# Expert trips of a two-layer feed-forward kernel: taken one batch at a time, spread over twelve steps, with a gelu built from tanh and GpSimd products

## The reference

```python
x = x + 0.5 * ffn(layernorm(x))      # stage 0
x = x + attention(layernorm(x))      # stage 1: relative position bias, 1024 x 1024 per head
x = x + 0.5 * ffn(layernorm(x))      # stage 2, same weights as stage 0

def ffn(x):
    x = x + attention_without_bias(layernorm(x) * ln1_w + ln1_b)
    y = layernorm(x) * ln2_w + ln2_b
    expert = argmax(y @ gate_w + gate_b)             # one of 8 experts per token
    return x + gelu_tanh(y @ w1[expert]) @ w2[expert]   # 128 -> 512 -> 128
```

## Time and profile before

| what | value |
|---|---|
| median of 3 runs | 2478.51 us (2477.31 to 2483.67) |
| the profiled execution, its time | 2486.23 us |
| its span | 2484.4 us |
| granted TensorE clock, mean | 0.924 of full speed |
| first to last exponential | 73.3 to 2368.4 us of the span |
| PE, DVE, ACT, POOL busy | 2179.9, 1935.1, 1910.1, 786.5 us (88%, 78%, 77%, 32%) |

### The profile page before, as it was taken

The page is one execution under the profiler, slowest core; times in us unless marked ns, Lnnn a source line. Parts: engine busy times, 40 slices in busy tenths (PEclk is TensorE's granted clock), DMA queues, the critical chain, the costliest instruction groups (busy, mean ns, idle before and its releaser), DMA issues. The chain is left out here.

```text
span 2484.4 us, 62352 instructions
## 1 busy us (share of the span) xinstructions
PE 2179.9 (88%) x24162; PEld 797.6 (32%) x24162; DVE 1935.1 (78%) x3222; ACT 1910.1 (77%) x3561; POOL 786.5 (32%) x1167
## 2 busy tenths in 40 slices
PE   5899988889997999999999899999889889988945
PEld 1222221225421334543233233222222223532435
DVE  7989898985788886578888888899989998569210
ACT  1788787889877777887777777788979988878822
POOL 1344634330634521042442023022061232062153
PEclk7899898899988999999999899899999999999967
DMA  4335433235304434743443333111101103622525
GB/s 112 98 104 151 127 82 90 54 91 160 83 23 110 124 99 143 214 117 93 113 115 99 101 98 102 48 36 28 39 23 42 36 15 102 173 65 60 139 78 145
DMA packets 269674, 231.91 MB, mean 93 GB/s; under 512 B 64241, under 2 KB 223857, under 8 KB 269346
## 3 DMA queue, kind: packets, MB, share of 16 engines
q1 hardware_dynamic: 258114, 219.54, 31.7%
q0 software_dynamic: 11264, 8.40, 1.9%
HBM read 175.35 MB, written 65.04 MB: 97 GB/s over the span
## 5 line engine op out<-in xcount | busy, mean ns | idle before, releaser
L1299 ACT ACTIVATE probs<-psum 128x512 f32<-128x512 f32 x3072 | 1619.1, 601 | 333.0 <-PE psum L1066 193.4
L1412 DVE TENSOR_REDUCE maxes<-psum 128x2 f32<-128x1024 f32 x1216 | 1422.5, 1215 | 267.8 <-PE psum L1034 257.2
L1103 PE MATMUL psum<-probs,v_ones 128*9 128x256 f32 (+1 forms) x11520 | 994.5, 419 | 0.0
L1066 PE MATMUL psum<-q_staged,k_staged 27*128 27x512 f16 x3072 | 809.4, 406 | 47.5 <-DMA q_staged<-neg_max 17.2
L1034 PE MATMUL psum<-k_staged,q_staged 24*128 24x512 f16 x3072 | 631.1, 409 | 160.0 <-DVE maxes L1412 124.1
L1417 DVE CUSTOM_DVE_ANT_0 biased<-psum,strips 128x512 bf16<-128x512 f32 x640 | 409.4, 686 | 103.3 <-PE psum L1034 86.4
L1034 PEld LDWEIGHTS psum<-k_staged,q_staged 24*128 24x128 f16 x3072 | 145.6, 92 | 901.5 <-DVE maxes L1412 510.4
L1103 PEld LDWEIGHTS psum<-probs,v_ones 128*9 128x9 f32 x11520 | 172.2, 89 | 332.4 <-issue 261.8
L1066 PEld LDWEIGHTS psum<-q_staged,k_staged 27*128 27x128 f16 x3072 | 222.2, 91 | 174.9 <-ACT probs L1299 84.7
L815 POOL TENSOR_SCALAR max_rest<-max_turned 128x32 f32<-128x32 f32 x96 | 28.3, 295 | 649.6 <-DVE max_turned L1455 647.4
L1086 PE MATMUL psum<-near,ident_b 64*64 64x256 bf16 (+4 forms) x3840 | 149.3, 251 | 0.0
(11 more groups left out here) (166 smaller groups left out, 1292.7 us busy)
## 6 DMA issues: line engine op xcount, KB each, us to landing
m_w<-in_w SPq DMA_DIRECT2D x204, 256.0 KB
near<-bias_near SPq DMA_DIRECT2D x128, 240.0 KB
strips<-bias_strips SPq DMA_DIRECT2D x64, 288.0 KB
k_staged<-k_parts SPq DMA_DIRECT2D x192, 48.0 KB
bias_cuts<-bias_window SPq DMA_DIRECT2D x32, 240.0 KB, 3.1
near<-bias_cuts SPq DMA_DIRECT2D x32, 240.0 KB, 3.7
bias_near<-near SPq DMA_DIRECT2D x32, 240.0 KB, 4.0
heads<-heads_t SPq DMA_DIRECT2D x384, 18.0 KB
```

The costliest lines, as they stand in the source:

```text
L1066: mm_ = pe.matmul(bank[:, :], k.kst[p][rows_, kt * P:(kt + 1) * P], queries, start=True, stop=not biased_)
L1103: last = pe.matmul(heads_bank[32 * j:32 * j + VC, columns], k.v[:, batch_of(u) * KT + kt, u % QUADS * 4 + j, :], probs[:, step % 3 * 4 + j ...
L1299: act.activation(probs[:, step % 3 * 4 + e % 4, :], bank[:, :], ACT.Exp, scale=unscale[is_mid(u)]).then_inc(taken, 1)
L1412: dve.reduce_max(maxes[u % 2][:, half, 2 * i:2 * i + 2, t, chunk], slot, AX.X).then_inc(drained, 1)
```

## The change

- Every batch of stages 0 and 2 is its own set: 8 sets of 5 trips, 40 trips in place of 34. The scatter target shrinks to 15 tiles, the normalised tokens to one batch.
- In the six sets other than the last two batches of stage 2, a trip takes 12 steps (`PITCH`). Its first-layer products come at steps 1, 3 and 5 of the trip, its second-layer products and their evictions one slot each at steps 7, 9 and 11, its weight loads at steps 6 to 8 and 12 to 14. First trips: step 117 for the first set, then 175, 239, 303, 623 and 687.
- In these trips gelu is no table function. ScalarE copies the hidden layer with a factor sqrt(0.044715); GpSimd forms x^3 + x in three instructions (`pool_cube`, one step later); ScalarE takes the tanh (`act_bend`, three steps after the copy); GpSimd multiplies and adds in two instructions (`pool_gelu`, four steps after the copy); the eviction scales by 0.25/sqrt(0.044715).
- The last two batches keep gelu and one-burst trips (`DIRECT`). The trips of batch 2 lie behind the last unit, at steps 768, 771, 776, 788 and 791; those of batch 3 stay at 810 and on.
- The gathers of stage 0 come at steps 179, 237, 301 and 365 (before: 203, 235, 331, 363); with them the projections of stage 1.
- The parts of a projection half (turn, q, k, v) come at 0, 2, 4, 6 in place of 0, 2, 3, 4. `pool_near` runs at 61, 77, 93 and 109. Two units of stage 1 lose their late loading (`LATE_UNITS`).

On ScalarE, in the second unit with trips of stage 0. The first rows are of before: a trip (m_yt, gelu m_hidden, m_out) with its two table loads.

The diff, cut to its core (the waits of the SyncE loads follow the new step tables and are left out):

```diff
-MT = 2 * KT + E
+MT = KT + E - 1
...
-BATCHES = {(0, 0): (0, 1), (0, 2): (2, 3), (2, 0): (0, 1), (2, 2): (2,), (2, 3): (3,)}
+BATCHES = {(n, b): (b,) for n in (0, 2) for b in range(B)}
...
+DIRECT = [(STAGES - 1, b) for b in (B - 2, B - 1)]
+PITCH = 12
+CUBE = 0.044715 ** 0.5
+BEND = (2 / math.pi) ** 0.5 / CUBE
...
-    return route_step(n, b) + FIRST_TRIP[len(BATCHES[n, b])] + (3 if len(BATCHES[n, b]) == 2 else 4) * trip
+    if (n, b) == DIRECT[0]:
+        return TRIPS_BEHIND[trip]
+    if (n, b) == DIRECT[1]:
+        return route_step(n, b) + FIRST_TRIP + 4 * trip
+    return route_step(n, b) + (FIRST_TRIP if (n, b) != SETS[0] else FIRST_SET_TRIP) + PITCH * trip
+
+def hidden_at(n, b, r):
+    return 1 if (n, b) in DIRECT else 1 + 2 * r
+
+def down_at(n, b):
+    return ((2, tuple(range(SLOTS))),) if (n, b) in DIRECT else tuple((7 + 2 * r, (r,)) for r in range(SLOTS))
...
-PROJECT_SINCE = {0: "p_turn", 2: "p_q", 3: "p_k", 4: "p_v"}
+PROJECT_SINCE = {0: "p_turn", 2: "p_q", 4: "p_k", 6: "p_v"}
...
-NEAR_STEPS = [8 * w + 5 for w in (WINDOWS - 1, WINDOWS + 2, WINDOWS + 5, WINDOWS + 7)]
+NEAR_STEPS = [8 * w + 5 for w in (WINDOWS - 1, WINDOWS + 1, WINDOWS + 3, WINDOWS + 5)]
...
+    def pool_cube(pool, n, b, trip, r):
+        x, power = hidden[r][:, :], bent[bend_index(n, b, trip, r) % 2][:, :]
+        pool.wait_ge(taken, seat["m_hidden", n, b, trip, r] + 1)
+        if bend_index(n, b, trip, r) >= 2:
+            pool.wait_ge(m_ready, bend_index(n, b, trip, r) - 1)
+        link(pool, pool.tensor_tensor(power, x, x, op=ALU.mult))
+        link(pool, pool.tensor_tensor(power, power, x, op=ALU.mult))
+        pool.tensor_tensor(power, power, x, op=ALU.add).then_inc(m_cubed, 1)
+
+    def pool_gelu(pool, n, b, trip, r):
+        x, curve = hidden[r][:, :], bent[bend_index(n, b, trip, r) % 2][:, :]
+        pool.wait_ge(m_bent, bend_index(n, b, trip, r) + 1)
+        link(pool, pool.tensor_tensor(curve, curve, x, op=ALU.mult))
+        pool.tensor_tensor(x, x, curve, op=ALU.add).then_inc(m_ready, 1)
...
+                if (n, b) not in DIRECT and since == 1:
+                    pool_cube(pool, n, b, trip, r)
+                if (n, b) not in DIRECT and since == 4:
+                    pool_gelu(pool, n, b, trip, r)
...
+    def act_hidden(act, n, b, trip, r):
+        bank = take(act, "m_hidden", n, b, trip, r)
+        if (n, b) in DIRECT:
+            act.activation(hidden[r][:, :], bank[:, :], ACT.Gelu_apprx_tanh).then_inc(taken, 1)
+        else:
+            act.activation(hidden[r][:, :], bank[:, :], ACT.Copy, scale=CUBE).then_inc(taken, 1)
+
+    def act_bend(act, n, b, trip, r):
+        act.wait_ge(m_cubed, bend_index(n, b, trip, r) + 1)
+        curve = bent[bend_index(n, b, trip, r) % 2][:, :]
+        act.activation(curve, curve, ACT.Tanh, scale=BEND).then_inc(m_bent, 1)
```

More of the change, by code:

```diff
@@ L172 @@
 LAST_STEP = gather_step(2, B - 1) + 8
-DOWN_STEPS = {trip_step(*key) + 2: [key] for key in TRIP_KEYS}
-LATE_UNITS = [(B + b) * QUADS for n, b in SETS if n == 0]
+DOWN_STEPS = {}
+for key in TRIP_KEYS:
+    for since, slots in down_at(*key[:2]):
+        DOWN_STEPS.setdefault(trip_step(*key) + since, []).append((*key, slots))
 class Core:
@@ L261, in taken_places @@
                 put("exp", u, e)
-        for n, b, trip in DOWN_STEPS.get(step, ()):
-            put("m_down", n, b, trip)
+        for n, b, trip, slots in DOWN_STEPS.get(step, ()):
+            put("m_down", n, b, trip, slots[-1])
         if u < UNITS:
@@ L283, in taken_places @@
                     put("m_turn", n, b, trip)
-                if since == 1:
-                    for r in range(SLOTS):
+                for r in range(SLOTS):
+                    if since == hidden_at(n, b, r):
                         put("m_hidden", n, b, trip, r)
@@ L399, in stages @@
     hidden = [k.sb(f"m_hidden{r}", [P, HID]) for r in range(SLOTS)]
+    bent = [k.sb(f"m_bent{p}", [P, HID]) for p in range(2)]
     expert_out = k.sb("m_out", [P, SLOTS, C])
@@ L1250, in pe_middle @@
     def pe_middle(pe, step):
-        for n, b, trip in DOWN_STEPS.get(step, ()):
-            pe_down(pe, n, b, trip)
+        for n, b, trip, down_slots in DOWN_STEPS.get(step, ()):
+            pe_down(pe, n, b, trip, down_slots)
     def pe_between(pe, step):
@@ L1378, in act_between @@
                                    scale=aff2[:, 0:1]).then_inc(taken, 1)
-                if since == 1:
-                    for r in range(SLOTS):
-                        bank = take(act, "m_hidden", n, b, trip, r)
-                        act.activation(hidden[r][:, :], bank[:, :], ACT.Gelu_apprx_tanh).then_inc(taken, 1)
+                for r in range(SLOTS):
+                    if since == hidden_at(n, b, r):
+                        act_hidden(act, n, b, trip, r)
+                    if (n, b) not in DIRECT and since == hidden_at(n, b, r) + 3:
+                        act_bend(act, n, b, trip, r)
+    def act_hidden(act, n, b, trip, r):
+        bank = take(act, "m_hidden", n, b, trip, r)
+        if (n, b) in DIRECT:
+            act.activation(hidden[r][:, :], bank[:, :], ACT.Gelu_apprx_tanh).then_inc(taken, 1)
+        else:
+            act.activation(hidden[r][:, :], bank[:, :], ACT.Copy, scale=CUBE).then_inc(taken, 1)
[3 more added lines that the diff above has]
+        act.activation(curve, curve, ACT.Tanh, scale=BEND).then_inc(m_bent, 1)
     def act_scales(act, mid):
@@ L1390, in act_middle @@
     def act_middle(act, step):
-        for n, b, trip in DOWN_STEPS.get(step, ()):
-            bank, done = take(act, "m_down", n, b, trip), trip_index(n, b, trip)
-            if done:
+        for n, b, trip, down_slots in DOWN_STEPS.get(step, ()):
+            bank, done = take(act, "m_down", n, b, trip, down_slots[-1]), trip_index(n, b, trip)
+            if done and down_slots[0] == 0:
                 act.wait_ge(m_stored, done * 16)
-            act.activation(expert_out[:, :, :], bank[:, 0:SLOTS * C].rearrange("p (r c) -> p r c", r=SLOTS),
-                           ACT.Copy, scale=0.5).then_inc(taken, 1)
+            run = slice(down_slots[0], down_slots[-1] + 1)
+            act.activation(expert_out[:, run, :], bank[:, :].rearrange("p (r c) -> p r c", c=C)[:, run, :],
+                           ACT.Copy, scale=0.5 if (n, b) in DIRECT else 0.25 / CUBE).then_inc(taken, 1)
     def dve_max(dve, u, m):
@@ L1761, in _ @@
                     pace(sp, step)
-                    for late in LATE_UNITS:
-                        if step == project_step(1, batch_of(late), 1) + STORE_SINCE + 2:
-                            for piece in range(len(UNIT_LOADS)):
-                                load_unit(sp, late, piece)
-                    if u + 2 < UNITS and u + 2 not in LATE_UNITS and t in UNIT_LOADS:
+                    if u + 2 < UNITS and t in UNIT_LOADS:
                         load_unit(sp, u + 2, UNIT_LOADS.index(t))
```

75 lines of the change are left out of this document (43 added, 32 removed).

## The result

| | before | after |
|---|---|---|
| median of 4 runs | 2480.66 us (2477.31 to 2483.67) | 2614.50 us (2610.38 to 2625.76) |
| ratio, 95% interval | | 1.0547 (1.0509 to 1.0585): slower |
| profiled execution: span, clock | 2484.4 us, 0.924 | 2615.3 us, 0.915 |

The forecast was 2503 us, 2448 to 2560: the direction was right, the loss of 134 us was put at 24. The first line of the page and the rows of table loads show that the change does what it says: GpSimd (POOL) is busy 1333.7 us instead of 786.5, and two table loads are left of 58.

A forecast was written before the change was run, and what follows sets the result against it. VectorE bounds quiet stage 2, TensorE quiet stage 1 and the bursts. -168.6 + 117 + 65 + 12 + 8 - 11 + 8 - 3 - 3 = +24.4 us gave 2503 us, range 2448 to 2560.

The forecast's parts named there:

- late deliveries of GpSimd: Cubes, gelu products and maxima splits miss their dates in the loop, stopping ScalarE or TensorE: +65 us.
- lock of VectorE: VectorE instructions with both inputs in SBUF, chiefly in five routings, shut out by GpSimd products: +12 us (0 to 25).
- near copy: Near-bias copies at step 77 make the normalisation due at 83 about 8 us late; with stops removed elsewhere, -11 together.
- SyncE's loads: SyncE's loads get more room in the changed order and no shorter deadline: 0 us.
- spread trips: ScalarE and TensorE work of 30 trips in the loop: 22 at 3.5 us, 8 in stage 1 at 5.0, +117.
- behind the last exponential: After the loop, heads_t moves ahead and trips fill idle time: -3 us (-8 to +6).
- bursts gone: Removing 29 burst trips from four TensorE-bound stretches, table loads included, saves 168.6 us, 5.8 a trip.
- the ends are 52 and 115: Bounds in us on GpSimd's lateness: work exceeding quiet time, or every late delivery charged in full; 65 taken.
- the content: GpSimd's work against the time its steps take where outputs or gathers meet trips: 52 us over.
- six places charged job by job: Stretches where GpSimd's jobs were laid out in order, each late delivery charged in full: 115 us.
- third rival: Spread trips no cheaper than bursts, 5.8 us each, since foreign instructions upset bank rotation: +57, 2560 us; chance 0.10.
- second rival: Each GpSimd lateness paid in full, 115 us, and VectorE's lock 25: 2566 us; chance 0.15.

The follow-up runs named there:

- experiment 1: Changed kernel without its 450 products on GpSimd: tanh in place on the copy, second layer waits for tanh alone; 2482.9 us, 1.0015 of before.
- experiment 5: Changed kernel with tanh one step later, gelu products one later, second layer, later weight loads and gathers two later; 2619.3 us, 1.0552 of before.
- experiment 7: Changed kernel with most of the first set's weight loads 15 steps later and the last set's behind its token loads; 2615.6 us, 1.0527 of before.
- experiment 8: Changed kernel with all 40 trips as bursts, gelu from the table, no products on GpSimd; 2496.7 us, 1.0068 of before.
- experiment 4: Changed kernel with a set's eight scatters at steps 17 to 21 instead of one a step at 13 to 20; 2623.4 us, 1.0575 of before.

## Why the prediction was wrong

| step of the prediction | put at | the runs |
|---|---|---|
| late deliveries of GpSimd | +65 | +113 (80 its own products, 33 its other jobs) |
| lock of VectorE | +12 | +18 |
| steps 60 to 117: near copy, one routing; SyncE's loads "0" | +11 | +29, with or without products |
| spread trips (25 of the 30: those of steps 175 to 367 and 623 to 751) | +102 with one routing | +124, experiment 1 over the prediction's quiet times |
| behind the last exponential | -3 | +11 |
| bursts gone | -168.6 | no run shows it by itself; 751 to 768: -20.8 against -25.3 |

- **The step that failed first** is "the ends are 52 and 115 ... VectorE can run two banks ahead of the others and takes some of it back; I take 65, nearer the content". The late deliveries measured 113. The six places charged job by job add up to 114, but that the sums meet is in part luck. In experiment 1 against the changed kernel, with the lock in it, the stretches with these places gave 28, 28, 9, 3, 9 and 11 us where 15, 40, 16, 4, 19 and 20 were charged, and the four stretches between them (217 to 239, 281 to 303, 665 to 687, 729 to 751), which the prediction charged with nothing, gave 35. TensorE waits for the gelu there too, 2 to 4 us at a time, though GpSimd has room: what is short there is the time from copy to second layer, and longer dates took half of the 35 away (experiment 5). Content over time is no estimate of that. The slower matmuls behind each stop had no term. Whether VectorE's two banks took something back is not shown.
- **The second** is "SyncE's loads get more room and no shorter deadline: 0". Room for the loads is not room in the queue: the first set's weight loads now stand between the loads and stores of two near copies, and cost the maxima 12.4 us at one step. Behind the last exponential the store of the trip at 791 and the weight loads stand ahead of the tokens, but mending that gave back only 1.6 us (experiment 7). The -3 there became +11 though heads_t went ahead as forecast: two more trips were to fill the idle time ahead of the last set's first turn, and TensorE still waited 15.7 us there (19.8 before); the first layer behind it took 4.7 us (5.4 before), so most of its -2.5 did not come. How much of the rest is the trips' own work stays open.
- **The spread trips** were mis-sized only: 4.9 us against 4.0 (17 at 3.5, 8 at 5.0), both over the same quiet times. The third rival's rule, a spread trip as dear as a burst, is too much: experiment 8 puts a burst 0.5 us above a spread trip.
- **Slips in the sum:** the loop of the kernel before holds 28 bursts, not 29, since the fifth trip of batch 2 has only its turn there: 6.0 us a trip, and 2567 for the third rival. The lighter places of GpSimd hold 68.5 us, not 69.5, which makes the content 48.
- **The lock** was right in kind; 18 us lie inside its bounds of 0 to 25.
- **Right:** the near copy at 77 (8.4 us against "about 8"), 2 table loads, GpSimd's 1334 us against 1360, the tanh and second layer as the ones who wait (117 us together). The second rival, all lateness and the lock at their upper ends, gave 2566; what it lacks is SyncE, the end and the trips' size.

The three items beside GpSimd, 18 + 14 + 22 us over their terms, and its own 54 make 108, where the miss is 110. Left out are steps up to 60, 4 us shorter, and 751 to 768, 5 longer than put. That last one is the clock of this execution: from 2470.00 to 2488.00 it was granted 0.50, and the same 122 matmuls that took 11.6 us at 1.00 in experiment 4 took 18.0; there the stretch was 37.7 us, not 45.0. What of the 29 us at steps 60 to 117 is neither the copy at 77 nor the stop at 111, some 8, was not tried; the routing of the first set, new there, and its scatters stand in these steps.

## What to carry to other kernels

An engine that is idle two thirds of the time is not a free one. With jobs that others wait for in a fixed order, work moved to it must be charged job by job, also where the engine has room, and a later date for one job can make the next one late. Move work off a busy engine only when the gain there (here 0.5 us a trip) is measured without the cost of where it goes. When a step is moved, its DMA issues move too; look at what stands behind them in the issuing queue.

## What the runs showed of the hardware

- A GpSimd fill of 128x512 in float32 took 0.53 us with the value 0.5, a product of that size 1.27, and 1.05 where both inputs were the same tile.
- A product on GpSimd stretched VectorE's row maxima from 175 to 266 ns in the mean, a fill to 183.
- After a wait of 7.7 us eight matmuls of 128x128 took 2.05 us at a granted clock of 0.50, and 1.13 at 1.00 where TensorE had waited 0.8.
- A weight load, whose address comes from a register, took 0.35 us of SyncE's queue by its row, but 1.4 and 1.7 us from the end of the issue before it (385.94 to 387.35, 388.68 to 390.38, of which 0.54 and 0.85 were the loading of the register); three in a row took 2.6 to 2.9.
